# One schedule table of an attention phase: where seven weightings stand among 26 tiles of scores

## The reference

```python
Qh = (Q @ W_q).reshape(b, lq, H, DK)            # lq = 4096, H = 8, DK = 16
Kh = (K @ W_k).reshape(b, lk, H, DK)            # lk = 3202
Vh = (V @ W_v).reshape(b, lk, H, DV)
scores = jnp.einsum('bqhd,bkhd->bhqk', Qh, Kh) * scale
attn = jax.nn.softmax(scores, axis=-1)
ctx = jnp.einsum('bhqk,bkhd->bqhd', attn, Vh).reshape(b, lq, H * DV)
X = Q + ctx @ W_o
ffn_out = jax.nn.relu(X @ w1.T + b1) @ w2.T + b2 + X
```

## Time and profile before

| | |
|---|---|
| median of 3 runs | 5905.83 us |
| profiled execution | 5899.1 us |
| its span | 5897.3 us |
| PE busy | 5487.9 us (93%) |
| DVE busy | 3786.7 us (64%) |
| ACT busy | 3161.4 us (54%) |
| POOL busy | 2632.6 us (45%) |
| first attention, scores, first to last start | 434.4 to 1712.3 us |
| ACT in front of an exponential, waiting for PE's score, both attentions | 1378.0 us |
| POOL in the first attention | 0 us |

### The profile page before, as it was taken

The page is one execution under the profiler, slowest core; times in us unless marked ns, Lnnn a source line. Parts: engine busy times, 40 slices in busy tenths (PEclk is TensorE's granted clock), DMA queues, the critical chain, the costliest instruction groups (busy, mean ns, idle before and its releaser), DMA issues. The chain is left out here.

```text
span 5897.3 us, 104136 instructions
## 1 busy us (share of the span) xinstructions
PE 5487.9 (93%) x28932; PEld 3449.5 (58%) x28932; DVE 3786.7 (64%) x6648; ACT 3161.4 (54%) x5849; POOL 2632.6 (45%) x1284
## 2 busy tenths in 40 slices
PE   5959999999979979999999999999999999699999
PEld 4834444444436746666565665656656665578877
DVE  4448887778856667777776777777767777322231
ACT  3327776667753336666666666666666665222222
POOL 0000000000000029999998999999989999000000
PEclk9969999999989979999999999999999999899999
DMA  3451111111123431111111111111111110422230
GB/s 100 123 126 27 35 33 32 33 35 34 29 87 107 125 98 37 32 40 39 40 39 31 38 38 41 40 39 28 40 40 40 38 29 21 133 82 86 69 99 22
DMA packets 328588, 325.58 MB, mean 55 GB/s; under 512 B 184625, under 2 KB 192689, under 8 KB 326065
## 3 DMA queue, kind: packets, MB, share of 16 engines
q1 hardware_dynamic: 328112, 319.92, 20.3%
HBM read 219.18 MB, written 100.53 MB: 54 GB/s over the span
## 5 line engine op out<-in xcount | busy, mean ns | idle before, releaser
L759 DVE TENSOR_REDUCE a_maxes<-a_mscore 128x1 f32<-128x458 f32 (+4 forms) x5632 | 3050.5, 604 | 1023.1 <-PE a_mscore L804 1019.9
L742 ACT ACTIVATE a_prob<-a_score 128x512 f32<-128x512 f32 x4992 | 2595.1, 604 | 1389.9 <-PE a_score L813 1378.0
L804 PE MATMUL a_mscore<-a_k,a_qm 96*128 96x458 f32 (+4 forms) x5632 | 2067.9, 414 | 67.9 <-DMA a_k<-k 54.5
L813 PE MATMUL a_score<-a_q,a_k 97*128 97x512 f32 (+1 forms) x4992 | 2053.0, 433 | 76.9 <-ACT a_prob L742 57.1
L712 POOL TENSOR_TENSOR a_added<-a_added,a_prob 128x1024 f32<-128x1024 f32 x768 | 1837.2, 2392 | 90.6 <-ACT a_prob L742 34.2
L804 PEld LDWEIGHTS a_mscore<-a_k,a_qm 96*128 96x128 f32 (+1 forms) x5632 | 1576.2, 309 | 215.1 <-DVE a_maxes L759 96.0
L832 PE MATMUL a_acc<-a_prob,a_v 128*32 128x512 f32 x9984 | 1610.0, 607 | 0.0
L813 PEld LDWEIGHTS a_score<-a_q,a_k 97*128 97x128 f32 (+1 forms) x4992 | 944.7, 193 | 1125.0 <-ACT a_prob L742 613.8
L709 POOL TENSOR_TENSOR a_added<-a_prob 128x1024 f32<-128x1024 f32 x128 | 305.4, 2386 | 2264.2 <-ACT a_prob L742 2263.7
L827 PE MATMUL a_acc<-a_prob,a_ones 128*1 128x512 f32 x2048 | 967.9, 595 | 0.0
L832 PEld LDWEIGHTS a_acc<-a_prob,a_v 128*32 128x32 f32 x9984 | 293.4, 109 | 244.5 <-issue 154.2
(11 more groups left out here) (187 smaller groups left out, 3792.3 us busy)
## 6 DMA issues: line engine op xcount, KB each, us to landing
a_qm<-q SPq DMA_DIRECT2D x384, 64.0 KB, 1.9
a_q<-q SPq DMA_DIRECT2D x384, 64.0 KB, 1.8
acc<-a_acc_sb SPq DMA_DIRECT2D x384, 64.0 KB
e_part<-acc SPq DMA_DIRECT2D x90, 256.0 KB, 3.4
a_k<-k SPq DMA_DIRECT2D x48, 416.0 KB, 5.9
q<-m_qout SPq DMA_DIRECT2D x128, 128.0 KB, 2.3
e_wo<-wo_split SPq DMA_DIRECT2D x32, 512.0 KB, 4.2
k<-kv_out SPq DMA_DIRECT2D x30, 512.0 KB, 2.7
```

The lines of the kernel that those rows point to most:

```text
L742: act.activation(prob[:, t], score[SCORES[it.j][t]][:], ACT.Exp, scale=SCALE).then_inc(exp_done, 1)
L759: dve.tensor_reduce(maxes[j][:, t, c:c + 1], mscore[u % UNIT_BANKS][:, 0:wide], AX.X, ALU.max).then_inc(unit_read, 1)
L804: pe.matmul(mscore[u % UNIT_BANKS][:, 0:wide], qm[j][r:r + ROW, t:NB:NB // P], kt[kk][r:r + ROW, at:at + wide], start=True, stop=True).the ...
L813: pe.matmul(score[SCORES[it.j][t]][:], kt[it.k][r:r + C, i * P:(i + 1) * P], qt[it.j][r:r + C, :], start=True, stop=True).then_inc(score_d ...
```

## The change

The table `at` of the first attention becomes one of tiles. The weightings stand behind tiles 0, 3, 11, 14, 17, 20 and 23, where they stood behind 1, 5, 9, 13, 17, 21 and 25. The units move with them: `more` gives the number of units behind a tile where it is not one (it may be none now). The second attention's tables are rewritten in the new form with the same meaning (pair 1 becomes tile 3, and so on), and its matmuls stand in the same order. So do all instructions of DVE, ACT, SP and POOL in both attentions.

```diff
-            self.at = {0: (5, True), 2: (6, True), 4: (0, False), 6: (1, False), 8: (2, False), 10: (3, False),
-                       12: (4, False)}
+            self.at = {0: (5, True), 3: (6, True), 11: (0, False), 14: (1, False), 17: (2, False), 20: (3, False),
+                       23: (4, False)}
             self.copy_at = 3
-            self.CHUNKS, extra, self.early = 8, {3: 2, 11: 2, 19: 2}, 16
+            self.CHUNKS, self.early = 8, 16
+            more = {0: 2, 1: 0, 3: 3, 8: 2, 9: 2, 12: 0, 14: 2, 17: 2, 18: 2, 22: 0, 23: 2}
...
         for t in range(ST):
-            more = 1 + extra.get(t, 0)
-            self.units_at.append(range(made, made + more))
-            made += more
+            self.units_at.append(range(made, made + more.get(t, 1)))
+            made = self.units_at[-1].stop
...
             for it in items(pe):
-                for s in range(GROUPS):
-                    if s == 0:
+                for t in range(ST):
+                    if t == 0:
                         pe.wait_ge(q_loaded[it.j], (it.use + 1) * LOADS)
                         pe.wait_ge(row_loaded[it.j], (it.use + 1) * 16 * HALVES)
-                    scores(it, 2 * s)
-                    due(it, 2 * s)
-                    scores(it, 2 * s + 1)
-                    due(it, 2 * s + 1)
-                    if s in L.at:
-                        b, last = L.at[s]
+                    scores(it, t)
+                    due(it, t)
+                    if t in L.at:
+                        b, last = L.at[t]
```

More of the change, by code:

```diff
@@ L457, in __init__ @@
             self.batches = [[0, 1], [2, 3], [4, 5], [6, 7], [8]]
-            self.at = {1: (3, True), 3: (4, True), 5: (0, False), 8: (1, False), 11: (2, False)}
+            self.at = {3: (3, True), 7: (4, True), 11: (0, False), 17: (1, False), 23: (2, False)}
             self.copy_at = 4
-            self.CHUNKS, extra, self.early = 7, {3: 1, 18: 1}, 10
+            self.CHUNKS, self.early = 7, 10
+            more = {3: 2, 18: 2}
         self.HALVES = P // self.ROWS
```

## The result

The kernel after the change takes 5860.43 us (median of 5 runs, 5856.64 to 5868.53), the kernel before 5897.56 (5 runs, 5893.44 to 5909.09). The ratio is 0.994, with a 95% interval from 0.9927 to 0.9953: faster by 0.6%, where 1.6% was forecast. The profiled execution took 5857.08 us, its span 5855.3, against 5899.1 and 5897.3.

A forecast was written before the change was run, and what follows sets the result against it. PE's handovers with ACT and DVE bound each first-attention item. 55 x 1.78 = 98, plus 2, less 8 for the clock: 92 us saved, 5807 profiled, median about 5812; likeliest case 5785 to 5840, with two rivals 5780 to 5865.

The forecast's parts named there:

- What bounds it: First attention only: handovers between PE and ACT and between PE and DVE bound an item; at most 1278 us can move.
- The short stretches: Five stretches, tiles 1-3, 12-14, 15-17, 18-20, 21-23: no ACT or DVE waits; 2.05 us with four units, 1.87 with three.
- The border and the gap: Tiles 24, 25 and next tile 0: 2.83 us; tiles 4-11, without a weighting, paced by ACT: 5.22 us.
- the five waits foretold in the gap: Tiles 4-11: PE would wait for ACT five times, as ACT sets the pace; no separate size.
- Which items gain: 55 ordinary items gain 1.78 us each; six head starts (new head, next keys/values loading, row late) gain 0; others 2 us.
- The clock: PE waits 1 to 3.5 us behind all six head starts; low clock there charged 8 us more.
- the third rival: Slower: the long gap of tiles 4-11 drops the clock in every item; chance 0.04.

The follow-up runs named there:

- gap_units_twice: The changed kernel with every unit matmul behind tiles 4 to 11 issued twice, ten more matmuls in the gap: 5835.47 us, ratio 0.9888.
- short_units_twice: The changed kernel with units behind tiles 13 to 20 issued twice, eleven more matmuls there and none in the gap: 5956.43 us, ratio 1.009.
- twice_early_row_first: The changed kernel with the four units behind tiles 4 to 7 issued twice and keys and values loaded after the row of maxima: 5853.23 us.
- gap_of_six: The changed kernel with weightings behind tiles 0, 3, 9, 12, 16, 19, 23, so the gap has six tiles and six units: 5949.62 us.
- the last kernel: The changed kernel with weightings behind tiles 2, 6, 10, 14, 18, 21, 24, units spread, acc copy later, keys after the row: 5778.58 us.

## Why the prediction was wrong

The sign was right, and the size was not: 37 us by the medians (42 in the profiled executions) where 94 (92) were forecast. Two sums in it are slightly off and change nothing: 5807 and 6.7 make 5814, not 5812, and short stretches all at 1.49 make the item 20.5, not 20.3.

1. *What bounds it.* Right: the second attention's scores span 2841 us before and 2842 after, and the gain lies in the first.

2. *The short stretches.* Right within 0.07 us each. Measured medians of undisturbed items are 2.02, 2.07 and 2.11 for the three-tile stretches with four units (2.05 predicted), 1.84 and 1.93 with three (1.87), and no wait for DVE is left (77.7 us, now 1.1).
3. *The border and the gap.* 2.90 against 2.83, and 5.28 against 5.22. Of the five waits foretold in the gap only two show as pauses of PE. Together with the others the item is 18.17 where 17.94 was predicted, and before it was 19.80 rather than the 19.72 of the one item that I read. The saving is 1.63, not 1.78: 90 us, not 98.
4. *Which items gain.* Right: head starts gained 0.9 us of 124.6, and the row was late at five places, not six, 8.0 us in all. Moving the row ahead of the keys took 7 us out of the head starts and left no wait for the row, which shows that it was the order of SP's issues.
5. *The clock.* **This step failed.** It charged 8 us, at head starts alone. No run shows this term. It was my estimate: the item of the earlier trace rows took 954.67 - 930.86 = 23.8 us, 4.1 more than the 19.72 of another, with 13.6 us at 0.50, which is 0.30 us for each us at 0.50 and 8.5 for the 28.2 us of the three stretches there; I charged about as much again. What the runs show in its place: the six head starts together took 123.7 us, where they had taken 124.6, and in the ordinary items the low clock adds 55 us more than before. The mechanism is that of the third rival, which I had given 0.04: the long gap drops the clock. gap_units_twice shows it by taking the falls away in the gaps of all ordinary items but one, short_units_twice by not doing so (41 in the gap), and twice_early_row_first by doing it in part (25 in the gap, where 36 were). The rival's argument against, that nine items with waits kept 1.00, was taken from items without a gap, so it did not bear on this one; its other one, 18 matmuls in 4.2 us, was no protection, since the clock fell with just these, 34 times. The rival also had two things wrong: a fall in every item, and a kernel slower than before. In fact 34 of 55 items hold low clock, mostly one stretch of 3.4 us, which costs 1.5, less than the 1.63 that an item saves. gap_of_six and short_units_twice show that it could have ended as the rival said: where the saving is smaller and the gap remains, the kernel is slower than before by 0.8 and 0.9%.

The account closes: 90 us from the items less 55 back to the clock, 0.9 from the heads and 1.6 from the first and last items make 37. Of the 5 us left of the 42, 1.3 lie ahead of the first attention, 2.9 between the two and the rest behind, where the order of work is unchanged.

What stays open is whether it is the pauses or the little work between them that counts in a gap. A short pause alone was not enough: in the gap PE's recorded pauses are 0.28 and 0.21 us, in the border stretch 0.40 with no fall there. But the work that cured the gap also filled its pauses, so they are not excluded as the cause inside it. Also open is why one ordinary item is hit and its neighbour, instruction for instruction the same, is not, as at 1428.98 and 1448.69. The rows of items at 20.5 us each in gap_of_six and short_units_twice say that more than the order of work within an item matters; no run here isolates it.

## What to carry to other kernels

When a reordering gathers one kind of heavy work elsewhere, look at what the matmul engine has left in the stretch it was taken from: here a gap of 18 matmuls in 4.29 us, with pauses of 0.28 and 0.21 us, cost 55 of the 90 us that the order saved in waits. Test that by adding harmless matmuls there (5835.47 us here, where the change takes 5860.43); if the kernel gets faster, spread the work instead (5830.52, and 5778.58 for the last kernel, both with the row ahead of the keys). And let a small store and reload that the next step waits for go ahead of bulk loads on its queue: that took the six head starts from 123.7 to 116.7 us here.

## What the runs showed of the hardware

- The granted clock fell to 0.50 for 3.4 us after a gap of 4.3 us in which PE was never recorded idle for more than 0.28 us, and more matmuls in the same place, which also filled the pauses, kept it at 1.00 in the gaps of all ordinary items but one (28 instead of 18, kernel time 5835.47 against 5860.43 us).
- Each us at 0.50 cost 0.43 us of time here, not 1 (61.5 us for 143.4): of 3.4 us of low clock, 1.5 came out as time. The trace of the kernel before gives 0.30 (4.1 us for 13.6).
- A low stretch was 3.4 us long in most gaps, but it could last: 44.4 us at 0.50 behind a head start of gap_of_six, with PE busy 43.69 of them.
- Items in a row each held a fall and each took about 20.5 us, though the undisturbed item of the same kernel took 19.07 (gap_of_six) or 19.47 (short_units_twice).
- The load of the row followed its store by 2.3 us with nothing between (751.63 to 753.90), and by 5.2 us with keys and values issued ahead of them (757.72 to 762.88), the store's own issue taking 2.44 instead of 0.36.
